# Last attention of a four-layer graph network: a third sum bank cleared by ScalarE, one key pass per quad, weight rows split between ScalarE and VectorE, and 30 units by matmul

## The reference

```python
z = h @ W_fc.T
z_src, z_dst, ex = z[src], z[dst], e @ W_edge.T
a = z_src @ blk[0] + z_dst @ blk[K] + ex @ w_e
for k in range(1, K):                       # moments over all edges: two constants
    a = a + src_m[k] @ blk[k] + dst_m[k] @ blk[K + k]
att = jnp.where(a > 0, a, SLOPE * a)
expv = jnp.exp(att - m[dst])                # m: maximum over the edges of a destination
w = expv / segment_sum(expv, dst)[dst]
msg = w[:, None] * (z_src + ex @ W_e2n.T)
return segment_sum(msg, dst)
```

## Time and profile before

| | us |
|---|---|
| median of 3 runs (1913.54 to 1918.93) | 1918.82 |
| profiled execution, its own time | 1916.29 |
| its span, first to last instruction | 1914.5 |
| first keys to last sum of the last attention's loop | 1457.9 to 1880.4 |
| mean granted TensorE clock, share of full speed | 0.837 |

### The profile page before, as it was taken

The page is one execution under the profiler, slowest core; times in us unless marked ns, Lnnn a source line. Parts: engine busy times, 40 slices in busy tenths (PEclk is TensorE's granted clock), DMA queues, the critical chain, the costliest instruction groups (busy, mean ns, idle before and its releaser), DMA issues. The chain is left out here.

```text
span 1914.5 us, 44162 instructions
## 1 busy us (share of the span) xinstructions
PE 1365.9 (71%) x12903; PEld 1155.2 (60%) x12903; DVE 1417.2 (74%) x3785; ACT 1007.7 (53%) x2221; POOL 1241.5 (65%) x1328
## 2 busy tenths in 40 slices
PE   4476676676676767677776478648676788898884
PEld 3355555555555555555555378638576778888784
DVE  5777777777777777777777788788855777777774
ACT  2454444454454454454454295039724677777771
POOL 1677777777777777777777186025537777777740
PEclk8678878878888888888888688869966999999996
DMA  6333333333333333333332221000232222223210
GB/s 102 99 77 82 83 76 83 82 76 83 81 77 82 82 77 82 82 77 82 83 77 74 65 58 60 4 1 2 86 82 51 61 61 60 62 61 71 62 21 18
DMA packets 125228, 128.65 MB, mean 67 GB/s; under 512 B 80959, under 2 KB 88435, under 8 KB 124840
## 3 DMA queue, kind: packets, MB, share of 16 engines
q0 software_dynamic: 35776, 62.74, 15.9%
q1 hardware_dynamic: 63778, 57.41, 9.9%
q10 hardware_dynamic: 25542, 6.81, 1.6%
HBM read 116.64 MB, written 10.20 MB: 66 GB/s over the span
## 5 line engine op out<-in xcount | busy, mean ns | idle before, releaser
L636 POOL DMA_INDIRECT shared<-kv_tab,idx x784 | 767.7, 979 | 289.7 <-issue 237.7
L839 PE MATMUL bank<-key_hot,lo_hot 128*128 128x350 f16 x784 | 185.0, 341 | 299.2 <-DVE count L700 245.9
L2284 POOL DMA_INDIRECT count<-att_tab,count x240 | 237.4, 989 | 111.4 <-issue 70.7
L839 PEld LDWEIGHTS bank<-key_hot,lo_hot 128*128 128x128 f16 x784 | 56.0, 98 | 386.4 <-issue 371.2
L700 DVE TENSOR_TENSOR count<-count,bank 128x350 f32 x392 | 205.2, 523 | 82.4 <-issue 43.2
L772 ACT ACTIVATE lo_dist<-iota_neg,tile_lo 128x128 f16<-128x128 f32 x784 | 238.5, 389 | 0.0
L685 DVE TENSOR_SCALAR key_hot<-iota_key,tile_key 128x350 f16<-128x350 f16 x784 | 196.1, 320 | 0.0
L706 DVE TENSOR_TENSOR prod<-bank,shared 128x512 f32<-128x512 f32 x98 | 67.7, 691 | 149.1 <-DMA shared<-kv_tab,idx 141.0
L2806 PE MATMUL bank<-shared 128*128 128x150 f32 x896 | 159.4, 327 | 1.8 <-DVE shared L2511 1.8
L2658 ACT ACTIVATE shared<-shared 128x126 f32<-128x126 bf16 x336 | 143.3, 483 | 31.2 <-PE bank L2806 25.1
L814 PE MATMUL bank<-webd,eaT 128*128 128x128 f32 x784 | 159.1, 368 | 0.6 <-ACT eaT L766 0.6
(11 more groups left out here) (528 smaller groups left out, 2974.7 us busy)
## 6 DMA issues: line engine op xcount, KB each, us to landing
shared<-in_edge_attr SPq DMA_DIRECT2D x97, 256.0 KB, 3.1
shared<-lo_tab SPq DMA_DIRECT2D x28, 512.0 KB
shared<-kv_tab,idx POOLq DMA_INDIRECT x784
count<-att_tab,count POOLq DMA_INDIRECT x240, 2.5
qwin<-q_tab ACTq DMA_DIRECT2D x196, 16.0 KB
kv_tab<-count SPq DMA_DIRECT2D x1, 1600.0 KB, 10.4
idx<-in_src SPq DMA_DIRECT2D x97, 4.0 KB, 1.6
g_edge<-att_tab,count POOLq DMA_INDIRECT x94
```

The costliest lines, as they stand in the source:

```text
L636: nc.gpsimd.indirect_dma_start(kv[:, s, c, :], None, kv_tab, bass.IndirectOffsetOnAxis(ap=idx[:, s, c:c + 1], axis=0)).then_inc(kv_in[s], 16)
L839: last = nc.tensor.matmul(bank[6 + q % 2][:, 0:KC], lo_hot[:, c, :], key_hot[:, c, :], start=i == 0, stop=i == GT - 1)
L2284: nc.gpsimd.indirect_dma_start(ring[s][:, j, 0:D + 2], None, att_tab[1], bass.IndirectOffsetOnAxis(ap=src_i[:, t:t + 1], axis=0)).then_inc ...
```

## The change

- A third bank: quads rotate over banks 2, 3 and 1. TensorE no longer clears them; ScalarE writes zeros into the bank (`clear_bank`, called first in `weights`) once the quad three before has been added, and TensorE waits for `bank_clear`. The limits test moves from bank 1 to the block sum's bank.
- `keys` makes the four tiles of a quad in one tensor_tensor of 128 x 600, with `iota_k` and the keys broadcast, in place of four tensor_scalars of 128 x 150. TensorE waits for it once a quad.
- Of a quad's four weight rows VectorE makes two (before: one) and ScalarE two (before: three).
- `ND` goes from 28 to 30, so 19 units are gathered in place of 21.

```diff
-ND = 28
+ND = 30
...
+        quad_banks = (2, 3, 1)
+        BY_ACT = QT // 2
...
                     if n >= LOW_RING:
                         dve.wait_ge(main_ok, n + QT - LOW_RING)
-                    last = at + QT - 1
-                    nc.vector.tensor_scalar(low_w[:, last, 0:FREE], iota[:, 0:FREE], lo_t[:, n + QT - 1:n + QT], cols_d[:, 1, s, (q + 1) * QT - 1:(q + 1) * QT],
-                                            ALU.is_equal, ALU.mult).then_inc(attr_ok, 1)
+                    for j in range(BY_ACT, QT):
+                        nc.vector.tensor_scalar(low_w[:, at + j, 0:FREE], iota[:, 0:FREE], lo_t[:, n + j:n + j + 1], cols_d[:, 1, s, q * QT + j:q * QT + j + 1],
+                                                ALU.is_equal, ALU.mult).then_inc(attr_ok, 1)
...
                     attributes(i, q)
-                    for n in range(i * UT + q * QT, i * UT + (q + 1) * QT):
-                        if n >= LOW_RING:
-                            dve.wait_ge(main_ok, n - LOW_RING + 1)
-                        nc.vector.tensor_scalar(keys_w[:, n % LOW_RING, :], iota_k, key_t[:, n:n + 1], None, ALU.is_equal).then_inc(key_ok3, 1)
+                    n = i * UT + q * QT
+                    at = n % LOW_RING
+                    nc.vector.tensor_tensor(keys_w[:, at:at + QT, :], bc(iota_k, 1, QT), bc(key_t[:, n:n + QT], 2, KH), ALU.is_equal).then_inc(key_ok3, 1)
...
-                    nc.vector.tensor_tensor(into, into, bank[2 + n % 2][:, 0:NT * QW].rearrange("p (h w) -> p h w", w=QW), ALU.add).then_inc(quad_added, 1)
+                    nc.vector.tensor_tensor(into, into, bank[quad_banks[n % 3]][:, 0:NT * QW].rearrange("p (h w) -> p h w", w=QW), ALU.add).then_inc(quad_added, 1)
...
-                    batch = range(i * UT + first, i * UT + first + QT - 1)
+                    clear_bank(i * (UT // QT) + first // QT)
+                    batch = range(i * UT + first, i * UT + first + BY_ACT)
...
+                def clear_bank(m):
+
+                    if m >= 3:
+                        act.wait_ge(quad_added, m - 2)
+                    nc.scalar.activation(bank[quad_banks[m % 3]][:, 0:NT * QW], zero_cols(NT * QW), ACT.Copy).then_inc(bank_clear, 1)
...
-                        if m >= 2:
-                            pe.wait_ge(quad_added, m - 1)
-                        into = bank[2 + m % 2]
-                        nc.tensor.matmul(into[:, 0:NT * QW], zeros_b[:, :], zero_cols(NT * QW), start=True, stop=False, skip_group_check=True)
+                        pe.wait_ge(bank_clear, m + 1)
+                        into = bank[quad_banks[m % 3]]
                         for j in range(QT):
                             n = m * QT + j
                             if j == 0:
-                                pe.wait_ge(attr_ok, 2 * (m + 1))
-                            pe.wait_ge(key_ok3, n + 1)
-                            if j < QT - 1:
-                                pe.wait_ge(low_ok, m * (QT - 1) + j + 1)
+                                pe.wait_ge(key_ok3, m + 1)
+                                pe.wait_ge(attr_ok, (QT - BY_ACT + 1) * (m + 1))
+                            if j < BY_ACT:
+                                pe.wait_ge(low_ok, m * BY_ACT + j + 1)
```

More of the change, by code:

```diff
@@ L2194, in build @@
         NPU = NU - ND
-        x_up, x_down, x_down2, z_even, z_odd, z_taken, v_ok, v_taken, vs_ok, vs_taken, win_ok, share_ok, share_used, turned_v, vc_ok = (
+        x_up, x_down, x_down2, z_even, z_odd, z_taken, v_ok, v_taken, vs_ok, vs_taken, win_ok, share_ok, share_used, turned_v, bank_clear = (
             short_sem(f"e_{n}") for n in ("x_turned", "x_copied_by_act", "x_copied_by_dve", "z_even", "z_odd", "z_taken", "v", "v_taken", "v_shifted", "v_shifted_copied", "windows", "share",
-                                          "share_used", "v_turned", "vc"))
+                                          "share_used", "v_turned", "bank_clear"))
         sum_z, sum_z_ok, mean_ok, mean_in, centre_ok, centre_in, centred, squared, cubed, power_ok, moment_ok, moved_m, log_in, root_ok, konst_in, konst_ok = (
@@ L2550, in choose @@
                     if i == CHECK_AT:
-                        nc.vector.tensor_reduce(lims[0:5, 8:9], bank[1][0:5, 96:96 + P], AX.X, ALU.max)
+                        nc.vector.tensor_reduce(lims[0:5, 8:9], bank[4 + 2 * (i % 2)][0:5, 96:96 + P], AX.X, ALU.max)
                         nc.vector.tensor_scalar(lims[0:5, 9:10], ident[0:5, 4:5], -1.0, 1.0, ALU.mult, ALU.add)
@@ L2555, in choose @@
                     if i == CHECK_AT + 1:
-                        nc.vector.tensor_copy(worst[0:1, 0:2], bank[1][0:1, 96:98])
+                        nc.vector.tensor_copy(worst[0:1, 0:2], bank[4 + 2 * (i % 2)][0:1, 96:98])
                         dve.drain()
@@ L2813, in check_limits @@
                         pe.wait_ge(lim_ok, 1)
-                        nc.tensor.transpose(bank[1][0:5, 96:96 + P], lim[:, 0:5], ident[:, :])
+                        nc.tensor.transpose(bank[4 + 2 * (i % 2)][0:5, 96:96 + P], lim[:, 0:5], ident[:, :])
                     if i == CHECK_AT + 1:
                         pe.wait_ge(lim_top, 1)
-                        nc.tensor.matmul(bank[1][0:1, 96:98], lims[0:5, 8:9], lims[0:5, 9:11], start=True, stop=True)
+                        nc.tensor.matmul(bank[4 + 2 * (i % 2)][0:1, 96:98], lims[0:5, 8:9], lims[0:5, 9:11], start=True, stop=True)
                 def gathered_sum(j):
@@ L2854, in _ @@
                     gathered_sum(j)
-        nc.clear_and_free_semaphores([x_up, x_down, x_down2, z_even, z_odd, z_taken, v_ok, v_taken, vs_ok, vs_taken, win_ok, share_ok, share_used, turned_v, vc_ok,
+        nc.clear_and_free_semaphores([x_up, x_down, x_down2, z_even, z_odd, z_taken, v_ok, v_taken, vs_ok, vs_taken, win_ok, share_ok, share_used, turned_v, bank_clear,
                                       sum_z, sum_z_ok, mean_ok, mean_in, centre_ok, centre_in, centred, squared, cubed, power_ok, moment_ok, moved_m, log_in, root_ok,
```

## The result

The changed kernel takes 1950.88 us in the median of 6 runs (1945.15 to 1954.49) against 1918.88 us of the kernel before (6 runs): the ratio is 1.0162, with a 95% interval of 1.0138 to 1.0185. It is 32 us slower. The forecast was 1932 us and its range ended at 1945; the sign was right, the size half of what came.

The account below looks back on a forecast made before the run. VectorE was taken to pace the last attention's loop. Units +18.0 us (with 0.10 off each), slow stretches -4, ScalarE's late work +2: +16 on 1916.3 gives 1932 us, range 1923 to 1941, 8 in 10 within 1916 to 1945.

Parts of the forecast that it names:

- The third bank: Before the fourth quad sum in the last attention's loop: VectorE's wait for TensorE goes, 28 x 0.62 = 17.4 us.
- the slow stretches: Parts of the loop at halved TensorE clock: waits there cost 7.9 us, of which the bank gives back 4.
- the late rows: ScalarE's weight rows for the fourth quad, queued behind its clear: just in time, 2 us allowed in all.
- another share of slow clock: Sign that the forecast is wrong: TensorE's clock halved for a different share than before; no size given.
- Rival A: ScalarE's new wait for the quad sum before its clear binds, with a clear of 1.0 us: 1946 us, chance 0.17.
- VectorE's own terms: Per quad on VectorE: one key pass saves 0.13 us, the second weight row adds 0.26, so it pays 0.13.
- The key pass: VectorE's one pass of 600 elements lasts 0.775 us and holds the engine 0.70, in place of 0.83 for four.
- C: Rival: the one key pass runs at two elements a cycle, holding VectorE 0.38 us: 1894 us, chance 0.06.
- the loss of 31 us: Skill's estimate for the key passes: 0.55 us for four old, 0.69 for the new, so fusing loses 0.13 a quad.
- The units: Loop with 30 matmul units in place of 28: 418.9 us after against 400.9 before, +18.0 us.
- The gathers: GpSimd's gathers, last one 31 us before the loop's end, do not set the pace; 32 less are worth nothing.

Follow-up runs that it names:

- TensorE's clear: Changed kernel with three banks and 30 units, but TensorE clears the banks with its matmul of zeros and ScalarE clears none: 1921.84 us, ratio 1.0021.
- the rows first: Changed kernel, but ScalarE makes a quad's two weight rows before it clears the bank: 1937.89 us, ratio 1.0098.
- The row alone: Changed kernel with TensorE clearing the three banks, 30 units, and VectorE making one weight row a quad in place of two: 1903.48 us, ratio 0.9926.
- 28 short units: Changed kernel with TensorE clearing three banks, one key pass, one weight row by VectorE, and 28 units in place of 30: 1936.79 us, ratio 1.0104.
- both mends together: Changed kernel with ScalarE's rows made before its clear and a matmul of zeros added on TensorE: 0.9879 and 0.9831 where the kernel before takes about 2650 us.

## Why the prediction missed

**The third bank: this step failed.** The prediction said that the fourth quad "can start when the keys are there, while VectorE makes two sums (1.7 us)", "so the 0.62 us goes: 28 x 0.62 = 17.4 us", and 4 us more from the slow stretches. With ScalarE's clear neither came. VectorE's four waits for TensorE in the loop (L2519, L2487, L2571, L2578) sum to 46.0 us, against 41.6 before; the prediction had them 19 lower. This is more than the whole miss of 16 us. With TensorE's clear both came nearly in full: 14.4 us in 57 waits, of which 11.4 are the gap of 0.20, so 3.0 us in place of 22.4.

Two causes are shown. The first is the late rows, a term that the prediction sized wrongly. The prediction had the row's path of 2.1 us right (1818.16 to 1820.30), and allowed 2 us in all for it. It set the fourth sum 3.1 us after the first sum's end and had "TensorE's last two or three matmuls between", but did not add them up. TensorE starts the quad 2.03 us after the first sum has ended (1818.13 to 1820.16), needs 1.29 us at the full clock, and VectorE starts 0.15 later, as in the run with the matmul added (1816.82 and 1.31, sum at 1818.28): 3.47 us. In the 14 units whose fourth quad ran at the full clock, the fourth sum started 3.47 to 3.50 us after that end; before it was 3.61 in most. So of the 0.5 us that the bank was to bring there, 0.13 came. The sum starts some 0.35 us late (0.55 in place of 0.20), 10 us in 30 units. With the rows first, the 0.55 us waits vanish.

The second is the clock. The prediction wrote off the 0.2 us that each matmul of zeros takes as "off the path", and named another share of slow clock only as a thing that would make it wrong, without price. The loop went from 0.93 to 0.86, and 16 fourth quads ran at the halved clock, against 5 such waits before, at about 1.05 us each: 17 us, of which the prediction had left 4. Adding the matmuls back, with no other use, took 9 of the 16 away in the profiled execution, and 14 us off the median. Closing the gap that ScalarE made left 5, in the shortest of its five executions. So the lost work feeds it, and the wait before the fourth quad most likely too; how the two shares divide is open. The Trainium skill (TensorE: Matmul & The Clock Gate, Part 1: The HAM clock gate) says that TensorE's clock follows how busy it has lately been. The run with the matmul added agrees: more work, and 0.91 in place of 0.86. The 3 us just ahead of a quad do not tell it, since 1.29 us busy came before a fall and 1.28 before none.

**Rival A** is the nearer to what came (1946 us), and its place was right, ScalarE's clear behind the first sum; that its time came near is luck. The clear takes 0.57 us in place of the feared 1.0, its path to the gathered exponents stayed hidden, as the forecast had it (ScalarE still waits 25.4 us for VectorE there), and no rival had the clock.

**VectorE's own terms** stand. The key pass lasts 0.776 us (forecast 0.775) and holds the engine 0.70 (1702.47 to 1703.17). Two rows take 0.52 us of step in place of 0.26. C falls with this. So does the loss of 31 us that the prediction worked out from the Trainium skill, since the four old passes held VectorE 0.83 us in place of the 0.55 of that estimate. One bound does not come out of the rows: 400 elements in 0.565 us, scaled to 600, give 0.85 us and not 0.65. And the bounds of pass, row and slow stretches, taken together, span 1916 to 1956 us, more than the stated 1923 to 1941. The row alone came to 18 us of 31 where the kernel before takes 1918, the rest having gone to waits. On the changed kernel, the loop's time beyond VectorE's waits for TensorE grew by 29 us (456.0 - 46.0, against 422.5 - 41.6), where the prediction's sum has 35; what made the 6 us is open.

**The units** were priced well: two less took 20 us of work out of the loop of the changed kernel, where 20 to 24 follow from the periods. That the whole time fell by 23 is in part luck, since 14.4 us of waits for gathered rows stand against it, and 8 us of the profiled difference lie outside the loop.

**The gathers** were misread, though it cost the forecast nothing. The prediction gave GpSimd 31 us to spare, from its last gather to the loop's end. But behind the last gathered unit VectorE still has two matmul units to do. What counts is the distance to the first use of the rows, and in the kernel before that is short:

```profile
1849.37 0.94 POOL L2284 DMA_INDIRECT g_edge<-att_tab,count  x1 [0.30 <-issue]
1852.79 0.18 DVE L2458 TENSOR_TENSOR shared<-g_edge,count 128x14 f32<-128x14 f32 x1
```

A gather there lands 2.5 us after its issue in the median, so these rows came about 1 us before they were used, and VectorE had once waited 1.3 us already. The gathers of the kernel before ended just in time: so a shorter unit alone could bring little at 28 units, as the run with 28 short units shows. In the changed kernel the last gather starts at 1813.9 (forecast 1808) and is used at 1884.2, and VectorE waits for none.

## What to carry to other kernels

Where one engine's queue sets the pace and another's clear is moved to a third, follow the data from the event that frees the buffer through all that is queued behind it, down to the last instruction of the consumer, and compare that with the slack. Work that looks free on TensorE may hold up its clock: before it is taken away, look at what fills the gaps ahead of the one matmul group that somebody waits for. Measure an engine's slack at the first use of what it delivers, not at the end of the loop: here 1 us, where the loop's end gave 31. And the split of units between two methods is to be set last: at 28 units the kernel with short units was slower (1.0104) than with 30 (0.9926).

## What the runs showed of the hardware that was not expected

- A matmul of 128 x 500 zeros, added before each of 120 quads and used by nobody, made the kernel 14 us faster, by way of TensorE's clock (0.86 to 0.91 in the loop).
- ScalarE writes 128 x 500 zeros to PSUM in 0.575 us, and holds its queue 0.51 to 0.53 of it.
- The same program took 1918 us on chip 3 and about 2650 on chips 1, 6 and 11; chip 3 too had 2670 for a time, and 1920 again later. In the long executions TensorE stands still between instructions that wait for nothing that the profile shows. The two stretches below are of one execution of 2614.68 us (both mends together); in the second TensorE is busy nearly all the time, at the full clock:

```profile
2098.00:2112.00 14.00, 2.27 (x18) 1.29 (x16) 4.48 (x11) 1.94 (x5) 8.84 (x10) 0.50 0.27 62
2118.00:2133.00 15.00, 14.28 (x184) 13.10 (x183) 11.91 (x34) 10.55 (x25) 0.04 (x1) 1.00 0.08 22
```

```profile
2103.55 0.19 PE L2780 MATMUL bank<-shared,ad_row 128*128 128x25 bf16 x1 [1.22 <-issue]
2104.96 0.18 PE L2780 MATMUL bank<-shared,ad_row 128*128 128x25 bf16 x1 [1.22 <-issue]
2105.67 0.22 PE L2780 MATMUL bank<-shared,ad_row 128*128 128x25 bf16 x2 [0.54 <-issue]
```

What delays the instructions there, gaps of 0.5 and 1.2 us, no run of this case shows.
